# Products that nobody reads between the sums of the last stage of a two-layer graph network

## The reference

```python
W = jnp.einsum('rb,bio->rio', comp, basis)            # 8 relations
h_all = jnp.einsum('ni,rio->nro', node_feats, W)      # messages
msgs = h_all[src, edge_types]                         # one row per edge
agg = jax.ops.segment_sum(msgs, dst, num_segments=n)
rgcn_out = agg + node_feats @ loop_w + h_bias
h = jax.nn.gelu(rgcn_out + node_feats, approximate=False)
out = layernorm(h) * ln_gamma + ln_beta               # added to x
```

## Time and profile before

| | us |
|---|---|
| median of 3 executions | 1618.47 |
| lowest and highest of them | 1613.39, 1624.01 |
| time of the profiled execution | 1609.75 |
| its span (first to last instruction) | 1607.9 |
| mean granted TensorE clock over the span, as a share of 2.4 GHz | 0.876 |
| last stage, first gather to the end of the span | 1017.46 to 1607.9 |

### The profile page before, as it was taken

The page is one execution under the profiler, slowest core; times in us unless marked ns, Lnnn a source line. Parts: engine busy times, 40 slices in busy tenths (PEclk is TensorE's granted clock), DMA queues, the critical chain, the costliest instruction groups (busy, mean ns, idle before and its releaser), DMA issues. The chain is left out here.

```text
span 1607.9 us, 18550 instructions
## 1 busy us (share of the span) xinstructions
PE 1168.3 (73%) x5463; PEld 864.7 (54%) x5463; DVE 908.4 (56%) x2801; ACT 454.6 (28%) x1150; POOL 889.5 (55%) x959
## 2 busy tenths in 40 slices
PE   5874579999899989999899988354565645553662
PEld 2443466777667766777667755233344424442452
DVE  5664577767777777777777662113434324533534
ACT  4652134443444443453444433000000000000000
POOL 2655656555555455555555510566676667666760
PEclk9997799999999999999999999687777767776776
DMA  6648666666667666566666611233343334433431
GB/s 203 157 132 265 208 200 201 205 222 202 207 197 233 206 210 188 189 223 189 203 191 220 194 46 57 79 108 106 113 125 114 114 106 121 119 115 109 121 114 51
DMA packets 137073, 255.68 MB, mean 159 GB/s; under 512 B 40426, under 2 KB 85460, under 8 KB 134026
## 3 DMA queue, kind: packets, MB, share of 16 engines
q0 software_dynamic: 50176, 154.19, 32.3%
q1 hardware_dynamic: 85834, 99.10, 19.0%
q10 hardware_dynamic: 960, 1.18, 0.2%
HBM read 192.76 MB, written 61.63 MB: 158 GB/s over the span
## 5 line engine op out<-in xcount | busy, mean ns | idle before, releaser
L1093 POOL DMA_INDIRECT arena<-qv_tab,srcs x392 | 391.8, 999 | 349.1 <-PE ps L1289 252.1
L1687 POOL DMA_INDIRECT arena<-h_all,typs x392 | 377.2, 962 | 210.3 <-issue 135.2
L1751 PE MATMUL ps<-arena 128*128 128x256 f32 x784 | 252.7, 482 | 114.8 <-DMA arena<-h_all,typs 49.9
L1289 PE MATMUL ps<-arena 128*128 128x264 f32 x784 | 221.2, 406 | 88.8 <-DVE arena L1437 49.9
L1751 PEld LDWEIGHTS ps<-arena 128*128 128x128 f32 x784 | 186.6, 246 | 176.1 <-issue 40.6
L1289 PEld LDWEIGHTS ps<-arena 128*128 128x128 f32 x784 | 140.2, 194 | 139.3 <-DVE arena L1437 66.8
L1500 DVE TENSOR_TENSOR arena<-arena,ps 128x512 f32<-128x512 f32 x196 | 134.3, 685 | 119.5 <-PE ps L1278 91.5
L1344 PE MATMUL ps<-wrel,arena 128*128 128x512 f32 x400 | 188.7, 598 | 1.7 <-ACT arena L1182 1.7
L1278 PE MATMUL ps<-arena 128*128 128x264 bf16 x1176 | 169.6, 282 | 12.6 <-DMA arena<-k_tab 11.0
L1278 PEld LDWEIGHTS ps<-arena 128*128 128x128 bf16 x1176 | 145.0, 145 | 41.4 <-issue 25.3
L1437 DVE TENSOR_TENSOR arena<-arena 128x512 f32<-128x512 f32 x196 | 134.0, 684 | 41.6 <-ACT arena L1150 40.9
(11 more groups left out here) (162 smaller groups left out, 1521.1 us busy)
## 6 DMA issues: line engine op xcount, KB each, us to landing
h_all<-arena SPq DMA_DIRECT2D x23, 1024.0 KB
arena<-dst SPq DMA_DIRECT2D x49, 256.0 KB
rel<-arena SPq DMA_DIRECT2D x77, 128.0 KB
arena<-k_tab SPq DMA_DIRECT2D x49, 198.0 KB
att<-arena SPq DMA_DIRECT2D x52, 132.0 KB, 6.0
qv_tab<-arena SPq DMA_DIRECT2D x25, 256.0 KB, 3.1
arena<-qv_tab,srcs POOLq DMA_INDIRECT x392
arena<-h_all,typs POOLq DMA_INDIRECT x392
```

Of the source, the lines that this page charges most:

```text
L1093: pool.indirect_dma_start(out=rowbuf[:, u * T + t, 0:2 * D], out_offset=None, in_=qv_tab, in_offset=bass.IndirectOffsetOnAxis(ap=srcs[:, v ...
L1289: last = nc.tensor.matmul(ps[:, AGG, 0:AW], ind[:, v % 2, t, :], rowbuf[:, v % 2 * T + t, D:2 * D + H], start=(t == 0), stop=(v == 0 and t ...
L1687: pool.indirect_dma_start(out=rowbuf[:, u * T + t, :], out_offset=None, in_=h_all[0:N * R, :], in_offset=bass.IndirectOffsetOnAxis(ap=typs ...
L1751: last = nc.tensor.matmul(ps[:, 6 + u, 0:D], ind[:, u, t, :], rowbuf[:, u * T + t, :], start=(t == 0), stop=(v == 0 and t == T - 1))
```

## The change

PE multiplies `ident` with the first 256 columns of `wout` into bank 3 after each pair of sums: two products after the pairs of t = 1 and t = 5, three after those of t = 3 and t = 7, ten in a window. No semaphore is waited for or incremented, and nobody reads bank 3.

```diff
+                def stay_busy(products):
+
+                    for _ in range(products):
+                        nc.tensor.matmul(ps[:, 3, 0:D], ident[:, :], wout[:, 0, :], start=True, stop=True)
+
                 def loop_part(m):
...
                         if t % 2:
                             last.then_inc(agg_done, 1)
+                            stay_busy(2 + t // 2 % 2)
```

## The result

| | before, us | changed, us |
|---|---|---|
| median of 8 executions each | 1619.28 | 1634.24 |
| profiled execution | 1609.75 | 1634.95 |
| its span | 1607.9 | 1633.1 |

The ratio is 1.0096, with a 95% interval of 1.0078 to 1.0113: slower by 15 us. The forecast was 1561. Nearest to it is the rival "the clock rises and the reports stay late" at 1622.

The account below looks back on a forecast made before the run. POOL's row of gathers, held up by late reports of PE's sums, bounds the last stage. Of 67.6 + 9.0 = 76.6 us, three quarters, 57.5, go: 1609.75 - 57.5 = 1552.3, plus 8.7 to the median, 1561; range 1535 to 1640.

Parts of the forecast that it names:

- the clock rises and the reports stay late: Last stage: clock rises, yet POOL still pauses every two windows; time as before plus some 4 us, 1622; chance 0.19.
- The undisturbed 490 us for the gathers: Last stage: 391 steps between POOL's gathers at 1.253 us each would take 490.0 us without pauses.
- the 67.6 us of extra waiting: Last stage: waiting within the 557.6 us from first to last gather, put down to late reports of PE's sums.
- Everything closes: Last stage: the whole 76.6 us of removable time goes, giving 1541.9; chance 0.16.
- Late reports go with a PE that is partly idle, not with this stage's code: Main premise, from last stage and attention stage: late reports accompany an idle PE; stated as a correlation.
- if the late reports go with the idle PE they go too: Last stage: fillers keep PE busy, so late reports vanish; at most 76.6 us can go, 57.5 expected.
- under 60 were forecast: Sign of being right: ACT's `take` has "remote" waits under 60 us in place of 286.5.
- an objection to one rival: Against all 76.6 us going: attention stage lacks sizeable late reports, but POOL gathers only 397 times in 700 us there.
- The forecast of its rise: Last stage: PE's clock goes from a mean of 0.73 to near 1.00, as in the attention stage.
- Fillers that fit behind the gathers: Two windows at full clock: PE needs 17.8 us with fillers against POOL's 20.05, leaving 2.2 us to spare.
- some 4 us: End of the last stage: fillers that the last window does in one piece, added where reports stay late.
- 5.5 us from the last gather to the end of `carry`: End of stage: 2.8 us for rows, then 0.86 sums, 1.3 fillers, 0.6 carry; before it was 14.5 us.

Follow-up runs that it names:

- Run 12: Kernel before, with a 128x256 memset on GpSimd after each gather, no fillers, on a late-report occasion: 1613.95 us, ratio 1.0018.
- run 10: Kernel before, with plain loads by SP replacing the indirect gathers, on a late-report occasion: 1408.53 us beside 1610.66.
- run 3: Kernel before, with a small POOL memset after each pair of gathers, no fillers, on a prompt-report occasion: 1506.86 us, ratio 0.9986.
- run 5: The changed kernel itself, measured again on a prompt-report occasion: 1516.67 us beside 1509.47 for the kernel before, ratio 1.0053.
- run 14: Changed kernel (ten fillers) plus a 128x256 memset after each gather, on a prompt-report occasion: 1587.73 us, ratio 1.0532 to the kernel before.
- run 9: Changed kernel with five fillers after each pair, twenty a window, on a late-report occasion: 1713.1 us, ratio 1.0595 to the kernel before.
- run 8: Changed kernel without fillers in the last four windows, on a late-report occasion: 1626.89 us, ratio 1.0061 to the kernel before.

## Why the prediction was wrong

- **What bounds the kernel.** Right. The undisturbed 490 us for the gathers, and that the 67.6 us of extra waiting are late reports, held: on prompt occasions the gathers take 495 us. "Everything closes" came to describe the kernel before on a prompt occasion: 1541.9 less the 33 us by which the stage starts earlier there is 1509. That is no merit of the change, which had no part in it.
- **The step that failed**: "Late reports go with a PE that is partly idle, not with this stage's code", and from it "if the late reports go with the idle PE they go too". With PE busy for 80% of the stage, `take` still had 301.3 us of "remote" waits, where under 60 were forecast. The late reports of a late occasion went with the indirect gathers following each other closely. Run 12 leaves the clock at 0.73 and PE idle for a third of the stage, and the reports are prompt; the changed kernel has PE busy and the clock at 1.00 around a report that is 9.4 us late; run 10 takes away the indirect gathers and the late reports go. The evidence for my step was two correlates that a third thing explained: in the attention stage the gathers are 2.1 us apart on average, because POOL waits for PE there; in its first 20 us they followed every 1.25 us. The prediction had this, as an objection to one rival, and should have weighed it against the main step. Its number there was a misreading: the 397 of the earlier trace rows are all of POOL's instructions, the gathers among them are 332.
- **Whose reports.** The prediction read them as reports of PE's products. They are wider than that. In the kernel before, PE itself is released late by DVE's indicators, which are finished at 1091.22:

```profile
1089.56 1.66 DVE L1795 TENSOR_SCALAR arena<-iotaj,arena 128x128 f32<-128x128 f32 x8
...
1098.57 2.93 PE L1751 MATMUL ps<-arena 128*128 128x256 f32 x6 [8.79 <-remote]
1099.44 0.38 ACT L1701 ACTIVATE arena<-ps 128x256 f32<-128x256 f32 x1 [14.49 <-remote]
1099.52 0.95 POOL L1687 DMA_INDIRECT arena<-h_all,typs  x1 [4.11 <-remote]
```

  The trace has the increment of the indicators' semaphore at 1098.53, 7.3 us after they end, in one bunch with PE's own to ACT and POOL. Five of the 49 windows start their sums 4.0 to 7.4 us late in this way.
- **The clock.** The forecast of its rise was right in direction (0.73 to 0.89 over the stage, 0.97 where reports were prompt). Its worth was rightly put at little: the gathers take 495.4 us at 0.79 and 495.1 at 0.97 (runs 3 and 5), 571.4 at 0.73 and 570.6 at 0.97 (runs 12 and 14). The prediction calls slices 25 and 26 a half-speed clock; the page has 0.6 and 0.8 there.
- **Fillers that fit behind the gathers.** The pitch and the sum were right: run 9 gave 26.0 us a cycle for 26.4 worked out, and on a prompt occasion ten fillers leave the gathers at 495 us. On a late occasion the slack is not free: after each late `take` PE must work off landed rows, an estimated 6.6 us to the last sum of a window with the fillers between at full clock (30 products at 0.216 us) instead of 3.6, and POOL waits for it (43.7 us by name against 20.1).
- **The end.** The rival had "some 4 us" for the last window. Measured 8.8 us in the profiles: 3.4 in the last window's sums and carry, and the rest in the windows before it, whose sums also start with their rows landed (run 8 takes the end back to 33.2 us). The forecast's own term, 5.5 us from the last gather to the end of `carry`, was mis-sized even for prompt reports: it is 16.1 us in run 5, since PE with its fillers has not caught up with POOL by then, and 5.7 in run 3 without them. So with all late reports gone the fillers would still have lost some 10 us at the end.
- **The report of a finished product.** On prompt occasions `take` follows `carry` by 0.04 us. On late ones it follows by up to 17.6 us (kernel before). The rule of the Trainium skill that I weighed ("PSUM — Partial Sum Buffer", section "Engine vs sequencer instructions": the increment fires when the matmul completes) agrees with the trace on prompt occasions alone; on late ones, as a statement of when others see it, the measurement decides against it.

## What to carry to other kernels

A correlation between two stages is not a cause: before building on "the engine is idle there", list everything else that differs between the stages, here the distance between gathers. A filler in an in-order stream is free only where the engine always waits for data that has yet to come; at the end, and after every stall, the real work stands behind it. And raise a clock only where the engine that it drives is the bound.

## What the runs showed of the hardware

- On late occasions increments by matmuls reached ACT, DVE and POOL up to 17.6 us late (a `carry` of the kernel before that ended at 1247.4 and a `take` at 1265.0), in order and in bunches, while GpSimd issued indirect gathers of 128 rows of 1 KB every 1.25 or 1.34 us. At 1.45 us, at 1.63 us, and with plain loads by SP they were prompt. Increments by other engines were mostly prompt (PE's `carry` at 1322.57 follows the end of ACT's `take` by 0.06 us), but not always: DVE's indicators released PE up to 7.4 us late. So it is not a property of matmuls.
- This happened on three occasions and not on four others, for the same program, with gathers at 1.25 us; it is worth 109 us of 1618. The attention stage has some 30 us of that: its last L1278 starts at 942.3 on a late occasion and at 911.7 on a prompt one:

```profile
L1278 PE MATMUL ps<-arena x1176: 275/276/428, 144.0 to 942.3; 128*128 128x264 bf16 x196
```

```profile
L1278 PE MATMUL ps<-arena x1176: 275/276/428, 143.4 to 911.7; 128*128 128x264 bf16 x196
```

  The first row is of the kernel before, the second of run 5. What sets the occasion, and by what path gathers hold up the increments, stays open. A page tells the two apart at a glance: for the gathers it gives a landing time on prompt occasions (median 2.8 us) and none on late ones, where records of increments are missing from the trace (for one semaphore of the gathers, 161 of 800 are there).
- A memset of 0.15 us on POOL is free between two indirect gathers: it runs in the 0.30 us after each.
